# Attention scores on TensorE: queries and keys in two f32r parts, two heads in the two halves of the rows

## The reference, cut to what matters

```python
xn = _layernorm(x)
# attention, 32 heads of 16, ALiBi, causal
qkv = einsum('bsd,od->bso', xn, w_qkv) + b_qkv
scores = einsum('bqhd,bkhd->bhqk', q, k) / sqrt(16)
scores = scores + slopes[:, None] * arange(1 - S, 1)
scores = where(causal, scores, -1e9)
out = einsum('bhqk,bkhd->bqhd', softmax(scores), v)
s = out @ w_out.T + b_out
# gated feed-forward of ternary octonion layers
g = silu(ffn(xn))
return x + s * g
```

## Time and profile before

| | us |
|---|---|
| median of 3 runs | 965.25 |
| lowest and highest | 963.32, 968.9 |
| the profiled execution's own time | 966.12 |
| its span, first to last instruction | 964.3 |
| PE busy in the span | 905.3 (94%) |
| VectorE busy | 648.4 (67%) |
| ScalarE busy | 462.2 (48%) |
| GpSimd busy | 110.8 (11%) |
| DMA queue of SP, share of 16 engines | 43.7% |

### The profile page before, as it was taken

How to read it: one execution, slowest core, us unless ns; L and a number is a source line. 1 busy time by engine, 2 the same in 40 slices (tenths; PEclk the granted TensorE clock), 3 DMA queues, 4 the chain that set the end, 5 groups by cost and what they waited for, 6 DMA issues and landing times.

```text
span 964.3 us, 16724 instructions
## 1 busy us (share of the span) xinstructions
PE 905.3 (94%) x5630; PEld 483.2 (50%) x5630; DVE 648.4 (67%) x1425; ACT 462.2 (48%) x634; POOL 110.8 (11%) x119
## 2 busy tenths in 40 slices
PE   3696999999999996999999999999999999999987
PEld 3582457645854682444444444444444444443565
DVE  5678543543454442774888888888888888883488
ACT  3474532243223311124666666666666666667610
POOL 1121212130313032120000000000000000000042
PEclk9798999999999998999999999999999999999999
DMA  7322004201410138911256664546664456742757
GB/s 199 148 83 77 1 25 154 85 1 38 164 60 0 58 139 119 126 17 44 41 75 102 100 84 73 78 72 100 95 86 74 77 74 100 99 134 102 246 180 306
DMA packets 78177, 92.41 MB, mean 96 GB/s; under 512 B 26829, under 2 KB 43213, under 8 KB 78129
## 3 DMA queue, kind: packets, MB, share of 16 engines
q1 hardware_dynamic: 78017, 91.54, 43.7%
q0 software_dynamic: 112, 0.27, 0.2%
HBM read 57.57 MB, written 33.82 MB: 95 GB/s over the span
## 4 chain that ended last, share of the span: by engine, by line
PE 51%; DMA 3%; DVE 3%; issue 2%; ACT 1%; SPq 1%; DVEq 0%; ACTq 0%
PE psum L1285 15%; PE psum L1256 14%; PE psum L1269 12%; PE psum L1274 3%; DMA o_scr<-osum 2%; PE psum L250 2%; PE psum L251 2%; PE psum L1259 1%; PE psum L262 1%; PE psum L261 1%; DMA r_scr<-den 1%; DMA Ks<-r_scr 1%; ACT hid L278 1%; SPq L1022 0%; DVE mx L1150 0%
## 5 line engine op out<-in xcount | busy, mean ns | idle before, releaser
L1100 ACT ACTIVATE probs<-psum 128x1024 f32<-128x1024 f32 (+1 forms) x256 | 222.1, 915 | 108.3 <-PE psum L1274 91.1
L1150 DVE TENSOR_REDUCE mx<-psum 128x1 f32<-128x512 f32 (+2 forms) x352 | 224.8, 685 | 37.9 <-PE psum L1256 26.2
L1256 PE MATMUL psum<-Ks,Qs 99*128 99x512 bf16 (+3 forms) x768 | 203.8, 329 | 7.9 <-issue 5.6
L1269 PE MATMUL psum<-Qs,Ks 102*128 102x512 bf16 (+3 forms) x768 | 190.4, 326 | 2.1 <-DVE g_stage L306 1.6
L1146 DVE CUSTOM_DVE_ANT_0 mshown<-psum,ahead 128x384 bf16<-128x384 f32 (+1 forms) x256 | 149.2, 621 | 33.1 <-PE psum L1256 32.0
L250 PE MATMUL psum<-X,MG 128*128 128x512 f16 (+1 forms) x352 | 136.3, 387 | 5.0 <-PEq L324 3.7
L251 PE MATMUL psum<-X,MG 128*128 128x512 f16 (+1 forms) x352 | 136.1, 387 | 0.0
L1256 PEld LDWEIGHTS psum<-Ks,Qs 99*128 99x128 bf16 x768 | 62.5, 97 | 134.9 <-DVE mx L1146 51.5
L1285 PE MATMUL psum<-probs,Vs 128*32 128x512 f32 (+3 forms) x1152 | 126.2, 521 | 0.0
L1269 PEld LDWEIGHTS psum<-Qs,Ks 102*128 102x128 bf16 x768 | 73.8, 98 | 57.0 <-ACT probs L1100 8.4
L278 ACT ACTIVATE hid<-psum,sig_scale 128x512 f32<-128x512 f32 (+1 forms) x44 | 30.2, 687 | 146.7 <-PE psum L251 146.6
(11 more groups left out here) (128 smaller groups left out, 1128.5 us busy)
## 6 DMA issues: line engine op xcount, KB each, us to landing
Qs<-q_scr SPq DMA_DIRECT2D x96, 128.0 KB
Ks<-k_scr SPq DMA_DIRECT2D x96, 128.0 KB
o_scr<-osum SPq DMA_DIRECT2D x32, 256.0 KB, 4.1
q_scr<-qk_stage SPq DMA_DIRECT2D x16, 384.0 KB, 2.4
k_scr<-qk_stage SPq DMA_DIRECT2D x16, 384.0 KB, 2.5
v_scr<-v_stage SPq DMA_DIRECT2D x16, 256.0 KB, 2.0
g_scr<-g_stage SPq DMA_DIRECT2D x16, 256.0 KB, 2.0
Vs<-v_scr SPq DMA_DIRECT2D x16, 256.0 KB
```

Source lines behind the costliest of these rows:

```text
L1100: nc.scalar.activation(probs[n % PSLOTS][:, 2 * pair:2 * pair + 2, 0:COLS[n]], s_bank[pair][:, :, 0:COLS[n]], ACT.Exp, scale=1.0 / INV_SCA ...
L1150: nc.vector.tensor_reduce(dst, m_bank[bank][:, 0:n * keys].rearrange("p (n k) -> p n k", n=n), AX.X, ALU.max).then_inc(max_read, 1)
L1256: last = nc.tensor.matmul(tile[:, hh, :], Qs[s][0:ROWS_MAX, h + hh, qb * P:(qb + 1) * P], Ks[s][0:ROWS_MAX, h + hh, k0:k0 + keys], start=( ...
L1269: last = nc.tensor.matmul(bank[:, at:at + cols], Ks[s][0:ROWS_ALL, 2 * pair + h, kb * P:(kb + 1) * P], Qs[s][0:ROWS_ALL, 2 * pair + h, (c ...
```

## The change

- q and k are kept as two f32r parts of 4 bytes each. ScalarE writes the high part, VectorE the low part in one instruction. The cast (L640) and GpSimd's `third` go. The store is 512 KB. The scratch tensors have two f32 parts.
- Three terms instead of six: 48 rows, +2 for the bias (50, `ROWS_MAX`), +2 for the maximum (52, `ROWS_ALL`). Heads 0 and 2 of a quad lie in partitions 0 to 51, heads 1 and 3 in 64 to 115 (`u` = 0, 1; `PAIRS` = 2).
- `scores` issues for each key block the matmul of u = 0 and at once that of u = 1, each into its own bank. The mask is added in two halves of 64 rows each (`r` = 0, 1), per half 64 columns a block.
- A maximum tile holds heads of one half alone, and tiles alternate between the halves. Tiles with 128 keys hold two heads, not four. There are 41 tiles, among them two of 128 keys that are masked on VectorE. A tile's mask is two matmuls.
- The maxima are split into two parts. The transpose is f32 and of all 128 rows. Two DMAs put the rows into the Q stack, two load the slopes, and the Q and K loads are 12 DMAs of 128 KB as before (3 terms x 2 x 2 halves).
- The bias parts are copied at the start from the input into the scratch tensor `a_scr`.
- `interleave` uses new costs: a score step counts its columns once.
- In `finish` the gated result stays in `osum`, so a later tile waits for the addition two tiles before.

```diff
-TERM_Q = [0, 0, 1, 1, 0, 2]
-TERM_K = [0, 1, 0, 1, 2, 0]
+TERM_Q = [0, 0, 1]
+TERM_K = [0, 1, 0]
 ROWS_QK = HD * len(TERM_Q)
-ROWS_MAX = ROWS_QK + 3
-ROWS_ALL = ROWS_MAX + 3
+ROWS_MAX = ROWS_QK + 2
+ROWS_ALL = ROWS_MAX + 2
+HALF = P // 2
+PAIRS = QH // 2
...
             keys = min(CH, P * (qb + 1) - CH * half)
-            n = CH // keys
-            for h in range(0, QH, n):
-                out.append((qb, h, min(n, QH - h), CH * half, keys))
+            n = min(CH // keys, PAIRS)
+            for pair in range(0, PAIRS, n):
+                out += [(qb, u, pair, n, CH * half, keys) for u in range(2)]
+            if half and keys == P:
+                out[-1:] = [(qb, 1, pair, 1, CH * half, keys) for pair in range(PAIRS)]
     return out
+
...
-        main += [("scores", 0, (n, pair), 2 * COLS[n] + 2 * P * len(STEPS[n][1]) * (n in DIAG)) for pair in range(2)]
+        main += [("scores", 0, (n, pair), COLS[n] + P * len(STEPS[n][1]) * (n in DIAG)) for pair in range(2)]
...
+                sp.dma_start(a_scr, alibi).then_inc(alibi_kept, 16)
...
-                def third(c):
-
-                    for m in range(2 * KT):
-                        pool.wait_ge(q2_done, c * 2 * KT + m + 1)
-                        nc.gpsimd.tensor_tensor(qk_stage[m % 2][:, 2, :], rest[m % 2][:], qk_stage[m % 2][:, 1, :],
-                                                ALU.subtract).then_inc(q3_done, 1)
...
-                        nc.vector.scalar_tensor_tensor(out=rest[m % 2][:], in0=bank_of(QK0 + m), scalar=bq_col[:, m:m + 1],
-                                                       in1=qk_stage[m % 2][:, 0, :], op0=ALU.add, op1=ALU.subtract).then_inc(evac_done, 1)
-                        dve.wait_ge(evac_done, evacuated(c, QK0 + m))
-                        nc.vector.tensor_copy(qk_stage[m % 2][:, 1, :], rest[m % 2][:]).then_inc(q2_done, 1)
+                        nc.vector.scalar_tensor_tensor(out=qk_stage[m % 2][:, 1, :], in0=bank_of(QK0 + m), scalar=bq_col[:, m:m + 1],
+                                                       in1=qk_stage[m % 2][:, 0, :].bitcast(f32), op0=ALU.add, op1=ALU.subtract
+                                                       ).then_inc(evac_done, 1)
...
+                            heads = scr[bass.ds(b, 1), part, bass.ds(hq * (QH * HD), QH * HD)].rearrange("a (p u d) t -> u d (a p) t", u=2, d=HD)
+                            for u in range(2):
+                                rows = slice(u * HALF + n * HD, u * HALF + (n + 1) * HD)
+                                sp.dma_start(dst[s][rows].bitcast(f32), heads[u]).then_inc(stacked[s], 16)
+
+                    slopes = a_scr[bass.ds(hq * QH, QH)].rearrange("(p u) r t -> u r p t", u=2)
+                    for u in range(2):
+                        sp.dma_start(Ks[s][u * HALF + ROWS_QK:u * HALF + ROWS_ALL].bitcast(f32), slopes[u]).then_inc(stacked[s], 16)
...
-                    sp.dma_start(Qs[s][ROWS_MAX:ROWS_ALL], mrows[:]).then_inc(m_stacked, 16)
+                    for u in range(2):
+                        sp.dma_start(Qs[s][u * HALF + ROWS_MAX:u * HALF + ROWS_ALL].bitcast(f32), mrows[u * QH * KB:(u + 1) * QH * KB]).then_inc(m_stacked, 16)
...
-                        nc.vector.tensor_copy(mrows[:], m_bank[bank][0:3 * QH * KB, 0:P // 2].bitcast(bf16)).then_inc(max_read, 1)
+                        dve.wait_ge(m_stacked, t * 32)
+                        nc.vector.tensor_copy(mrows[:], m_bank[bank][0:2 * QH * KB, 0:P]).then_inc(max_read, 1)
...
-                    nc.vector.tensor_scalar(mparts[:, 0, :], flat, -1.0, None, ALU.mult).then_inc(max_step, 1)
+                    nc.vector.tensor_scalar(high, found, -1.0, None, ALU.mult).then_inc(max_step, 1)
                     dve.wait_ge(max_step, t * MSTEP + 2)
-                    nc.vector.scalar_tensor_tensor(out=mrest[:], in0=flat, scalar=-1.0, in1=mparts[:, 0, :], op0=ALU.mult,
+                    nc.vector.scalar_tensor_tensor(out=low, in0=found, scalar=-1.0, in1=high.bitcast(f32), op0=ALU.mult,
                                                    op1=ALU.subtract).then_inc(max_step, 1)
-                    dve.wait_ge(max_step, t * MSTEP + 3)
-                    nc.vector.tensor_copy(mparts[:, 1, :], mrest[:]).then_inc(max_step, 1)
-                    dve.wait_ge(max_step, t * MSTEP + 4)
-                    nc.vector.tensor_tensor(mparts[:, 2, :], mrest[:], mparts[:, 1, :], ALU.subtract).then_inc(max_step, 1)
...
-                        if n >= 2:
-                            dve.wait_ge(gated_done, n - 1)
+                        if n >= 2 + (NCH - 1) * TT:
+                            dve.wait_ge(last_done, n - 1 - (NCH - 1) * TT)
+                        elif n >= 2:
+                            dve.wait_ge(fin_done, n - 1)
...
+                        nc.tensor.transpose(m_bank[bank][:, 0:P], mparts[:].rearrange("p f u r n -> p (f u r n)").bitcast(f32), identf[:]
                                             ).then_inc(max_filled, 1)
...
-                    qb, h, n, k0, keys = MAXT[i - (i > ROWS_AT)]
-                    masked = k0 + keys == (qb + 1) * P and n > 1
+                    qb, u, pair, n, k0, keys = MAXT[i - (i > ROWS_AT)]
+                    masked = masked_tile(qb, k0, keys) and n > 1
+                    rows, half = slice(u * HALF, u * HALF + ROWS_MAX), slice(u * HALF, (u + 1) * HALF)
                     tile = m_bank[bank][:, 0:n * keys].rearrange("p (n k) -> p n k", n=n)
                     for hh in range(n):
-                        last = nc.tensor.matmul(tile[:, hh, :], Qs[s][0:ROWS_MAX, h + hh, qb * P:(qb + 1) * P], Ks[s][0:ROWS_MAX, h + hh, k0:k0 + keys],
+                        last = nc.tensor.matmul(tile[:, hh, :], Qs[s][rows, pair + hh, qb * P:(qb + 1) * P], Ks[s][rows, pair + hh, k0:k0 + keys],
                                                 start=(hh == 0), stop=not masked and hh == n - 1)
                     if masked:
-                        last = nc.tensor.matmul(tile[:, :, keys - P:], identb[:], causal[:].unsqueeze(1).to_broadcast([P, n, P]), start=False, stop=True)
+                        for r in range(2):
+                            last = nc.tensor.matmul(tile[:, :, keys - P:], unit[half, r], causal[half, r].unsqueeze(1).to_broadcast([HALF, n, P]),
+                                                    start=False, stop=(r == 1))
                     last.then_inc(max_filled, 1)
...
-                    for h in range(2):
-                        bank = s_bank[pair][:, h, :]
-                        for kb, at, cols in blocks:
-                            last = nc.tensor.matmul(bank[:, at:at + cols], Ks[s][0:ROWS_ALL, 2 * pair + h, kb * P:(kb + 1) * P],
-                                                    Qs[s][0:ROWS_ALL, 2 * pair + h, (c + 1) * CH - cols:(c + 1) * CH], start=(at == 0), stop=n not in DIAG)
-                        if n in DIAG:
-
-                            squares = bank.rearrange("p (a q) -> p a q", q=P)[:, 0:blocks[-1][1] // P + 1:max(blocks[-1][1] // P, 1)]
-                            last = nc.tensor.matmul(squares, causal[:], identb[:].unsqueeze(1).to_broadcast([P, len(blocks), P]), start=False, stop=True)
+                    for kb, at, cols in blocks:
+                        for u in range(2):
+                            rows = slice(u * HALF, u * HALF + ROWS_ALL)
+                            last = nc.tensor.matmul(s_bank[pair][:, u, at:at + cols], Ks[s][rows, pair, kb * P:(kb + 1) * P],
+                                                    Qs[s][rows, pair, (c + 1) * CH - cols:(c + 1) * CH], start=(at == 0), stop=n not in DIAG)
+                    if n in DIAG:
+                        apart = max(blocks[-1][1] // P, 1)
+                        for r in range(2):
+                            for u in range(2):
+
+                                half = slice(u * HALF, (u + 1) * HALF)
+                                squares = s_bank[pair][:, u, :].rearrange("p (a q) -> p a q", q=P)[:, 0:(len(blocks) - 1) * apart + 1:apart, r * HALF:(r + 1) * HALF]
+                                last = nc.tensor.matmul(squares, causal[half, r], unit[half, 0, 0:HALF].unsqueeze(1).to_broadcast([HALF, len(blocks), HALF]),
+                                                        start=False, stop=(r == 1))
                     last.then_inc(s_filled, 1)
```

112 lines of the change are left out of this document (59 added, 53 removed).

## The result

| | before | after |
|---|---|---|
| median, us | 965.21 | 1002.97 |
| lowest and highest of 4 runs | 963.32, 968.9 | 995.55, 1005.2 |
| ratio, 95% interval | | 1.037 (1.031 to 1.044) |
| the profiled execution, its span | 966.12, 964.3 | 1005.2, 1003.4 |
| mean granted TensorE clock | 0.980 | 0.938 |

The changed kernel is 3.7% slower, where 954 was forecast. In four of the kernels further down (`unroll`, `rows3_unroll`, `start_fill`, `before_mended`) one execution stood apart from the others, at 990.9, 974.8, 974.4 and 1832.9 us, and no argument rests on these. The first view is the page: PE's busy tenths and its granted clock in 40 slices, and two DMA queues, of the kernel after.

A forecast was written before the change was run, and what follows sets the result against it. TensorE, without slack, was taken as the bound, with VectorE only 4.7 us per quad behind. Terms -7.7 - 1.5 - 0.5 - 2.0 + 1 = -10.7 gave 954 us; forecast case 940 to 965 (50%), overall range 917 to 982.

The forecast's parts named there:

- The quad: Attention, one quad of four heads: 28.4 us after the change, 0.55 less than now, bounds 27.4 to 29.2.
- The third rival: Attention's products: the two row halves do not overlap, TensorE needs 31.8 to 32.4 us a quad, about 1004 us; 14%.
- the second one's serial weights: Second rival, attention: halves' weights load one after the other and rows come late, quad 29.3, 968 to 978 us; 19%.
- TensorE's own sum of 25 us: TensorE's work per attention quad: 28.95 - 3.1 (scores) - 1.0 (maxima) + 0.1 (transpose) = 25 us, bounds 23 to 27.3.
- Fourteen quads run at this pace: Attention, quads 0 to 13: each takes 28.4 us, together -7.7 us.
- I take 0.5: Maximum rows at each quad's start: two DMAs replace one, costing 0 to 0.8 us, taken as 0.5, partly hidden.
- PE arrives no later: Each quad's start: SP's second DMA costs 0.3 to 0.8 us more while TensorE arrives no later.
- a wait of over 1 us at each quad: Sign that the forecast is wrong: a wait of over 1 us for the rows of maxima at each quad.
- Chunk 0, "-2.0": Chunk 0, VectorE continuous: a cast goes from some six tiles in that part, 6 x 0.34 = -2.0 us.
- GpSimd's third part: Chunks other than 0: cast and GpSimd's third part go at no gain, since they hid behind a full TensorE.
- The early tiles, "+1": Last chunk's early tiles, some 17 groups: changes of shape cost 0 to 0.2 us each, 0 to 3.4, taken as +1.
- quads 14 and 15: End of attention: quad 14 -1.5 us (fewer VectorE steps, faster TensorE before it), quad 15 -0.5 us (no maxima).

The follow-up runs named there:

- unroll: Changed kernel with TensorE's loop over four times three quads written out, so no branch back stands between quads: 984.4 us, ratio 1.021.
- rows3_unroll: Changed kernel with the rows of maxima at item 3, not 5, and TensorE's loop written out: 964.3 us, ratio 0.997.
- start_fill: `rows3_unroll` plus unused products at the attention's start: 8 before the first score product, 3 before each of the first six: 956.7 us, ratio 0.988.
- before_mended: Kernel before with the rows of maxima at item 3 and TensorE's loop written out: 967.8 us, ratio 1.001.
- same_rows: `rows3_unroll` with score products, maximum products and masks of both heads all on rows 0 to 63; results wrong: 1436.2 us, ratio 1.487.
- start_lean: `start_fill` with one unused product, not three, before each of the first six score products: 954.8 us, ratio 0.986 to the kernel before.
- scores_low: `rows3_unroll` with only both heads' scores and their masks on rows 0 to 63, scores contracting over rows 0 to 51: 1038.7 us, ratio 1.072.
- scores_all: `scores_low` with one line altered, score products contracting over rows 0 to 115: 1118.8 us, ratio 1.155 to the kernel before.
- the fillers: Changed kernel with five unused products in each quad's starting pause, on 128 rows (997.6 us) or on rows 0 to 63 (995.9 us).
- before_loop6: Kernel before with TensorE's loop made of two times six quads, not four times three: 978.1 us, ratio 1.012.
- fill: Changed kernel with five unused 128-row products at each quad's start, ahead of the wait for the rows of maxima: 997.6 us, ratio 1.032.

## Why the prediction was wrong

**What was right.** The quad. The forecast was 28.4 us. Its sum has 0.8 for the rows of maxima, although its text takes 0.5 for them; without them 27.6. Measured: 27.85 without the pause, 28.9 with it. VectorE 23.8 busy in a quad (forecast 23.3 back to back, and 4 to 5 idle); PE 27.0 of 28.9, 93% where "some 90%" was said; the pairs' starts within 0.02 us. The third rival (no overlap) is out, the second one's serial weights too; of the second, the half that came is the rows' lateness. The third rival's "about 1004" lies one microsecond from the measured 1003 by luck alone: it had TensorE full at 31.8 to 32.4 us a quad. In TensorE's own sum of 25 us the bounds "23 to 27.3" do not follow from the terms, which give 21.9 to 29.6; nothing further on uses them.

**The step that failed: "Fourteen quads run at this pace".** It gave -7.7 us where the runs have +41.7 (4.5 in quad 0, 37.2 in the 13 after it). It took for granted that TensorE's clock would stay at the 1.00 of the earlier trace rows. That row has PE busy 28.95 of 28.95. The change takes that fullness away, and nothing in the prediction asked what a TensorE with pauses does. In quads 1 to 13 there were 74.9 us at 1.2 GHz and 7.7 us of branch pauses beyond the 1.1; their 413.5 us are 37.8 above 13 x 28.9, so the lower clock cost 30 us, 0.4 for each of its microseconds. The Trainium skill, "TensorE: Matmul & The Clock Gate", section "HAM oscillation — how this bites in real kernels", describes a kernel whose clock falls again and again because TensorE waits for data between bursts of matmuls; our rows agree in kind, with ten falls behind waits. It explains it by idleness, and `same_rows` (300 of 300 us busy at 0.50) doesn't fit that as the records count busy time.

**The rows of maxima, "I take 0.5".** SP's second transfer cost what the prediction said (0.5 later). But its cost was taken as a shift of 0.5 us, some of it hidden by tiles in the banks. Measured is a pause of 1.1 us and a quad 1.05 longer (28.9 to 27.85): TensorE, faster through the quad's last part, also arrives earlier. "PE arrives no later" was the wrong side to look at. The text did name a wait of over 1 us at each quad as what would make it wrong; it came.

**Not seen at all: the loop's length.** The masks stand in two halves now (48 mask products beside a quad's 48 score products, L1298), and TensorE's loop body grew by 201 instructions. Instructions on an engine with work in front of it were costed at nothing. At the branch they cost 3.5 to 3.9 us three times, and falls behind it.

**Chunk 0, "-2.0".** In the earlier trace rows PE waits 7.20 us for L709; after, the waits of PE from 60 to 100 us have this:

```profile
PE psum L838 <- DVE wnat L717: 1.3, 1, 1.3
```

That wait is 5.9 us shorter, and from the first feed-forward product to the product behind it the kernel takes 4.95 us where it took 11.86: 6.9 us gained for 2.0 forecast. (The other 2.9 of the 9.8 in the account lie ahead of it, at the start, where the first feed-forward product comes anywhere from 70.6 to 73.8 us in the profiles of both sorts of kernel.) The cast is only part of it. GpSimd's third part, for which the prediction counts no gain, shows in VectorE's time: of the 64 instructions of L702 (TENSOR_SCALAR, 64x340) four take 1.18 to 1.19 us, and these are the four beside which an L521 runs on GpSimd; the other 60 take 0.23 to 0.25. After, all 64 take 0.25 at most. Timeline of the kernel before, then of the one after:

```profile
64.51 1.17 POOL L521 TENSOR_TENSOR qk_stage<-rest,qk_stage 128x512 bf16<-128x512 f32 x1 [5.07 <-DVE qk_stage L640]
```

```profile
63.05 4.13 DVE L710 TENSOR_SCALAR MG<-wnat 64x340 f16<-64x340 bf16 x16
```

The same 16 instructions took 5.06 us in the earlier trace rows. That it is the two engines side by side is read from this coincidence alone. Four times 0.94 us is 3.8 us of VectorE, more than the casts' 8 x 0.34.

**The early tiles, "+1".** The lead of 9.8 us holds through chunks 1 to 3, and at the first score product 3.8 are left: 6.0 us lost where +1 was taken and +3.4 was the upper end. Some 4 of them go in one place, the last of the 17 groups. The kernel before has one maximum tile there (434.04) and no wait; the changed one has four, for three banks:

```profile
425.93 0.38 PE L272 MATMUL psum<-MD,shared 80*128 80x512 f16 x1
426.24 0.66 PE L1274 MATMUL psum<-Ks,Qs 50*128 50x384 f32 x3
428.35 0.50 PE L1274 MATMUL psum<-Ks,Qs 50*128 50x512 f32 x1 [1.44 <-DVE mx L1161]
428.78 0.39 PE L271 MATMUL psum<-MD,shared 128*128 128x512 f16 x1
```

The fourth waits for a read that stands behind VectorE's L316, and the clock is down from 429.2 to 432.6. The change of shape shows as well: the first tile starts 0.31 us behind the feed-forward product ahead of it in 16 of 17 groups, where it was 0.21 to 0.22. That is 0.1 us a group on the way in, 1.6 in all. The Trainium skill, "TensorEngine Tiling (Array Packing)", section Key Properties, which the prediction cites, has TensorE drain at a change of tiling mode. These 0.1 us agree with it in kind. An f32r weight load that shows, for which the prediction has 0.11 us, would look the same, and no run parts the two.

**Quad 0 and the end.** -0.55 was forecast for quad 0. From the first score product to the next copy it lost 4.5 us, with the clock down for 6.8 us from 449.7 on; the rest of the table's +7.3 belongs to the early tiles. `start_fill` and `start_lean` bring part of it back. A pause of 1.57 us ahead of the first score stood in the kernel before too, with no fall behind it; the changed kernel has a second one of 0.41 us, 1.6 us later. For quads 14 and 15 -2.0 was forecast, and from the copy of quad 14's rows to the end the kernel takes 1.2 us more; why is open.

**What stays open.** Why this kernel's clock falls behind shorter pauses than the bf16 one's: for its short gaps, or for its products. Nothing points to the rows in use, by `scores_low` against `scores_all` and by the fillers. And why the clock is down for 85 us, and in `same_rows` for 935, with TensorE busy. The f32r products' exposed weight loads are a candidate: TensorE's records overlap them, so "busy" may hide stretches in which the array multiplies nothing. That is argued, not shown. That the branch's pause is the fetching of instructions is likewise read from its place, from the body's length and from the queue's bytes (0.43, 0.90 and, unrolled, 0.74 MB), not measured by itself: in `unroll` 0.74 MB cost no pause, and in `before_loop6` 0.75 came with two.

## What to carry to other kernels

When a change takes work off an engine that was never idle, look for what it will wait for next, at each loop boundary and each hand-off; on TensorE a wait costs its own length and may cost the clock for several times as long. Look at the granted clock per stage before the busy shares. A change that looks like a loss may be one that was left half done: here two edits of a few lines in the order of the work, and 14 products that nobody uses at the start of attention, turned +3.7% into -1.4%. And work taken off an engine that seemed to cost nothing can have held up its neighbour: see what else was slow beside it.

## What the runs showed of the hardware that was not expected

- A TensorE loop body of 1,530 instructions branched back in 0.21 to 0.24 us; one of 1,731 took 3.8 to 4.4, one of about 3,060 3.8 and a second pause of 3.5 us. Written out, the same work had no such pause.
- More TensorE work made a kernel faster: 26 and 14 unused products at the start of attention, -8 and -10 us. 80 in the quads' pauses (`fill`) took 16.7 us off the 13 quads; the whole kernel's -5 us is within the intervals.
- A granted clock of 0.50 for 935 us with TensorE busy in every window that was read.
- Falls of the clock behind pauses of 1.1 us in the changed kernel; none behind 14 pauses of 1.33 us in the bf16 one.
- f32r products on 116 rows follow each other at 0.34 us where those on 52 rows follow at 0.24 (512 columns, both heads on the same rows, clock 1.00 in both).
- A VectorE instruction of 0.25 us took 1.19 each of the four times that GpSimd's L521, of 1.17 us, ran beside it.
